# The experts' token rows turned on VectorE, in squares of 32 rows by 32 features written across partition groups, in place of TensorE transposes

## The reference

```python
# x: (2048, 512); 8 experts, 2 picked per token; hidden width F = 1024
x = x + gnn(layernorm(x), adj, ...)            # 2048 x 2048 masked softmax attention
Xf = layernorm(x)                              # (2048, 512)
router_w = softmax(Xf @ Wr)                    # 8 experts
topk_w, topk_idx = top_k(router_w, 2); topk_w = softmax(topk_w)
shared = (silu(Xf @ Wg_s) * (Xf @ Wu_s)) @ Wd_s
gate = silu(einsum('td,edf->etf', Xf, Wg)); up = einsum('td,edf->etf', Xf, Wu)
eout = einsum('etf,efd->etd', gate * up, Wd)
x = x + shared + einsum('etd,te->td', eout, w_full)
```

## Time and profile before

| | |
|---|---|
| median of 3 runs | 1418.66 us (1418.54 to 1420.81) |
| the profiled execution: its time / its span | 1418.73 us / 1417.1 us |
| TensorE busy | 1405.7 us, 99% of the span |
| VectorE busy | 746.4 us, 53% |
| ScalarE busy | 459.2 us, 32% |
| GpSimd busy | 189.5 us, 13% |
| mean granted TensorE clock | 0.999 of full speed (2.4 GHz) |

### The profile page before, as it was taken

How to read it: one execution, slowest core, us unless ns; L and a number is a source line. 1 busy time by engine, 2 the same in 40 slices (tenths; PEclk the granted TensorE clock), 3 DMA queues, 4 the chain that set the end, 5 groups by cost and what they waited for, 6 DMA issues and landing times.

```text
span 1417.1 us, 20076 instructions
## 1 busy us (share of the span) xinstructions
PE 1405.7 (99%) x7084; PEld 1215.3 (86%) x7084; DVE 746.4 (53%) x1557; ACT 459.2 (32%) x732; POOL 189.5 (13%) x234
## 2 busy tenths in 40 slices
PE   8999999999999999999999999999999999999998
PEld 7888888888888888898999889898898989888886
DVE  7955656656666577543243425234252526167874
ACT  4521222221222235343243424334242435243321
POOL 3500111211121133011001010101101010100000
PEclk9999999999999999999999999999999999999999
DMA  5811222322223256272617134261335353553101
GB/s 184 245 38 62 95 75 74 100 85 74 74 78 107 75 181 236 91 221 48 198 30 216 25 74 162 45 201 30 98 133 125 107 131 114 132 159 104 46 15 60
DMA packets 90517, 154.03 MB, mean 109 GB/s; under 512 B 11120, under 2 KB 29552, under 8 KB 88384
## 3 DMA queue, kind: packets, MB, share of 16 engines
q1 hardware_dynamic: 74160, 121.96, 25.5%
q0 software_dynamic: 9760, 18.93, 7.1%
q10 hardware_dynamic: 6528, 12.22, 3.3%
HBM read 114.09 MB, written 40.04 MB: 109 GB/s over the span
## 4 chain that ended last, share of the span: by engine, by line
PE 97%; DVE 1%; DMA 1%; issue 0%; ACT 0%; SPq 0%; POOL 0%; DVEq 0%; ACTq 0%; POOLq 0%
PE bank L279 91%; PE bank L778 2%; PE bank L801 1%; PE bank L982 1%; PE bank L931 1%; PE bank L795 0%; DMA early_x<-x2t 0%; PE bank L727 0%; PE bank L938 0%; DMA wq_raw<-in_L_gnn_W_q_dram 0%; DVE z L1786 0%; SPq L417 0%; PE bank L809 0%; DVE A_l L1396 0%; DVE xq_l L1396 0%
## 5 line engine op out<-in xcount | busy, mean ns | idle before, releaser
L1746 DVE TENSOR_TENSOR hid<-bank,hid 128x384 f32<-128x384 f32 (+1 forms) x80 | 46.7, 584 | 253.4 <-PE bank L279 253.4
L279 PE MATMUL bank<-dn_h,hT_h 128*128 128x512 f32 x416 | 167.9, 404 | 3.2 <-DVE hT_l L1396 3.2
L279 PE MATMUL bank<-dn_h,hT_l 128*128 128x512 f32 x416 | 163.7, 394 | 0.0
L279 PE MATMUL bank<-dn_l,hT_h 128*128 128x512 f32 x416 | 163.2, 392 | 0.0
L279 PE MATMUL bank<-xq_h,gate_h 128*128 128x384 f32 (+1 forms) x320 | 111.3, 348 | 0.1
L279 PE MATMUL bank<-xq_h,gate_l 128*128 128x384 f32 (+1 forms) x320 | 111.2, 347 | 0.0
L279 PE MATMUL bank<-xq_l,gate_h 128*128 128x384 f32 (+1 forms) x320 | 110.8, 346 | 0.0
L279 PE MATMUL bank<-xq_h,up_h 128*128 128x384 f32 (+1 forms) x320 | 110.7, 346 | 0.0
L279 PE MATMUL bank<-xq_h,up_l 128*128 128x384 f32 (+1 forms) x320 | 110.5, 345 | 0.0
L279 PE MATMUL bank<-xq_l,up_h 128*128 128x384 f32 (+1 forms) x320 | 110.4, 345 | 0.0
L279 PE MATMUL bank<-v_h,pT_h 128*128 128x512 f32 x256 | 103.7, 405 | 0.5 <-DVE pT_l L1396 0.5
(11 more groups left out here) (268 smaller groups left out, 3038.0 us busy)
## 6 DMA issues: line engine op xcount, KB each, us to landing
adj_t<-in_adj_dram SPq DMA_DIRECT2D x16, 1024.0 KB, 5.5
gate_raw<-in_L_ffn_Wg_dram SPq DMA_DIRECT2D x16, 1024.0 KB, 6.3
up_raw<-in_L_ffn_Wu_dram SPq DMA_DIRECT2D x16, 1024.0 KB, 9.6
dn_raw<-in_L_ffn_Wd_dram SPq DMA_DIRECT2D x16, 1024.0 KB, 11.5
x_t<-in_x_dram SPq DMA_DIRECT2D x24, 256.0 KB, 7.0
slots<-x2row ACTq DMA_DIRECT2D x12, 512.0 KB, 4.3
e_x<-slots ACTq DMA_DIRECT2D x22, 256.0 KB, 2.8
acc<-x SPq DMA_DIRECT2D x16, 256.0 KB, 2.0
```

What stands on the lines that cost most here:

```text
L279: mm = pe.matmul(o, lhs(a, c), rhs(b, c), start=first and n == 1, stop=last and n == 3 * len(chunks))
L1746: dve.tensor_tensor(hid[:, c % 2, 0:w], bank[2 + c % 2][:, 0:w], hid[:, c % 2, 0:w], ALU.mult).then_inc(sem("hid"), 1)
```

## The change

The transposes L931 of the blocks 1 to 7 (21 tiles) and all of L938 leave TensorE. VectorE turns the rows in squares instead: one instruction reads 32 partitions (rows 32i to 32i+31) and 4 x 32 features of a tile, and writes 32 partitions (32a to 32a+31) of `xq_raw` or of a new tile `tail_raw`. It takes 16 of them, over all (i, a), to turn a tile. In the blocks 2 to 7 the tiles 0 and 1 are turned together, 8 instructions of twice the length in each of the chunks 0 and 1, and tile 2 in the chunks 3 to 6, four instructions in each. In block 1, tile k is turned in the chunks 2+2k and 3+2k, eight in each, and the first tail tile's 16 stand in chunk 1. In a tail tile VectorE begins with the 16 squares of the next one. The copies that followed (`xq_h`, `xq_l`, `tail_xT_h`, `tail_xT_l`) now read SBUF, and stand in other chunks. The wait for `added` moves to the first square. Block 0 still turns its three tiles on TensorE.

```diff
-                return {3: 0, 5: 1, 7: 2}.get(c)
-            return {5: 0, 6: 1}.get(c) if b + 1 < BLOCKS else None
+                return ({4: (0,), 6: (1,), 7: (2,)} if b == 1 else {2: (0, 1), 7: (2,)}).get(c, ())
+            return {5: (0,), 6: (1,)}.get(c, ()) if b + 1 < BLOCKS else ()
+        SQUARES = [(i, a) for i in range(4) for a in range(4)]
+        def turned_in(b, c):
+            if b == 1 and c >= 2:
+                return (c - 2) // 2, 1, SQUARES[c % 2 * 8:][:8]
+            if 1 < b < E:
+                if c < 2:
+                    return 0, 2, SQUARES[c * 8:][:8]
+                if 3 <= c <= 6:
+                    return 2, 1, SQUARES[4 * (c - 3):4 * (c - 2)]
+            return 0, 0, []
+        def tail_turned_in(b, c):
+            return SQUARES if b == 1 and c == 1 else []
...
# TensorE, expert_block
-                    k = prepared_in(b, c)
-                    if k is not None and b + 1 < FIRST_SHARED:
-                        ...
-                        turn_rows(HEAD * b + k, (c + 1) % 2 if b == 0 else 7)
-                    if b == 1 and c == TAIL_IN:
-                        wait(pe, "xq_l", prepared(1) + 2)
-                        turn_tail(1)
+                    if b == 0 and c >= 5:
+                        wait(pe, "silu", c)
+                        turn_rows(c - 5, (c + 1) % 2)
# TensorE, tail_tile
-                if b < E:
-                    wait(pe, "xq_l", prepared(b + 1))
...
                 down(0, range(2, 4))
-                turn_tail(t + 1)
                 down(1, range(0, 4)).then_inc(sem("tail_down"), 1)
# ScalarE: the copies of the high parts read xq_raw and tail_raw; tail_tokens(1) in chunk 2
+                wait(act, "tail_up1", t)
                 tail_tokens(t + 1)
# VectorE
             def next_tokens(b, k, c):
-                    wait(dve, "added", 16 * adds(b - 1) if b > 0 else 0)
...
+            def turn_square(o, rows_, i, a, n=1):
+                return dve.transpose(o[32 * a:32 * a + 32, :, :].rearrange("p c (k q) -> p k c q", k=n)[:, :, :, 32 * i:32 * i + 32],
+                                     rows_[32 * i:32 * i + 32, :, :].rearrange("p k (c f) -> p k c f", c=DC)[:, :, :, 32 * a:32 * a + 32])
+            def turn_rows(b, k, n, squares):
+                for i, a in squares:
+                    if (i, a) == SQUARES[0]:
+                        for q in range(HEAD * b + k, HEAD * b + k + n):
+                            dve.wait_ge(sem(f"e_x_in{q % 2}"), 16 * (q // 2 + 1))
+                        wait(dve, "added", 16 * adds(b - 1))
...
+            def turn_tail(t, squares):
+                    if (i, a) == SQUARES[0]:
+                        wait(dve, "tail_x_in", 16 * t)
+                        wait(dve, "tail_xT_l", t - 1)
...
# VectorE, expert_block
+                    turn_rows(b, *turned_in(b, c))
+                    turn_tail(1, tail_turned_in(b, c))
+                    for k in prepared_in(b, c):
                         next_tokens(b, k, c)
-                    if b == 1 and c == TAIL_IN:
+                    if b == 1 and c == 2:
                         tail_tokens(1)
                     for u, k in todo[1:]:
                         piece(u, k)
# VectorE, tail_tile
+                turn_tail(t + 1, SQUARES)
                 for f in range(2):
```

More of the change, by code:

```diff
@@ L931, in turn_rows @@
                     mm = pe.transpose(bank[to][:, c * P:(c + 1) * P], e_x[:, q % 2, c * P:(c + 1) * P], ident[:])
[L932 to L939, removed]
+                mm.then_inc(sem("x2_turned"), 1)
             def expert_block(b, tail=None):
@@ L1268, in next_tokens @@
                     q = HEAD * b + k
-                    act.wait_ge(sem("rows_turned"), q + 1)
-                    copy(o[:, :, k * P:(k + 1) * P], bank[(c + 1) % 2 if b == 0 else 7][:].rearrange("p (c q) -> p c q", c=DC)
-                         ).then_inc(sem("xq_h"), 1)
+                    part = slice(k * P, (k + 1) * P)
+                    if b == 0:
+                        act.wait_ge(sem("x2_turned"), NT + q + 1)
+                        copy(o[:, :, part], bank[(c + 1) % 2][:].rearrange("p (c q) -> p c q", c=DC)).then_inc(sem("xq_h"), 1)
+                    else:
+                        act.wait_ge(sem("rows_turned"), q + 1 - HEAD)
+                        copy(o[:, :, part], xq_raw[(b + 1) % 2][:, :, part]).then_inc(sem("xq_h"), 1)
                     q += 2
@@ L1759, in next_tokens @@
                 if b + 1 < FIRST_SHARED:
-                    wait(dve, "added", 16 * adds(b - 1) if b > 0 else 0)
                     part = slice(k * P, (k + 1) * P)
-                    minus(o["l"][:, :, part], bank[(c + 1) % 2 if b == 0 else 7][:].rearrange("p (c q) -> p c q", c=DC),
-                          o["h"][:, :, part]).then_inc(sem("xq_l"), 1)
+                    raw = (bank[(c + 1) % 2][:].rearrange("p (c q) -> p c q", c=DC) if b == 0
+                           else xq_raw[(b + 1) % 2][:, :, part])
+                    minus(o["l"][:, :, part], raw, o["h"][:, :, part]).then_inc(sem("xq_l"), 1)
                 else:
@@ L1766, in next_tokens @@
                     minus(o["l"][:, part, :], xq_raw[(b + 1) % 2][:, part, :], o["h"][:, part, :]).then_inc(sem("xq_l"), 1)
+            def turn_square(o, rows_, i, a, n=1):
[7 more added lines that the diff above has]
+                        wait(dve, "added", 16 * adds(b - 1))
+                    q = HEAD * b + k
+                    if n == 2 and q % 2:
+                        rows_ = e_x[:, ::-1, :]
+                    else:
+                        rows_ = e_x[:, q % 2:q % 2 + n, :]
+                    ins = turn_square(xq_raw[(b + 1) % 2][:, :, k * P:(k + n) * P], rows_, i, a, n)
+                    if (i, a) == SQUARES[-1]:
+                        ins.then_inc(sem("rows_turned"), n)
+            def turn_tail(t, squares):
+                tail_rows = tail_x[:].rearrange("p (k d) -> p k d", k=1)
+                for i, a in squares:
+                    if (i, a) == SQUARES[0]:
+                        wait(dve, "tail_x_in", 16 * t)
+                        wait(dve, "tail_xT_l", t - 1)
+                    ins = turn_square(tail_raw[:], tail_rows, i, a)
+                    if (i, a) == SQUARES[-1]:
+                        ins.then_inc(sem("tail_turned"), 1)
             def tail_tokens(t):
                 wait(dve, "tail_xT_h", t)
-                minus(tail_xT["l"][:], bank[7][:].rearrange("p (c q) -> p c q", c=DC), tail_xT["h"][:]).then_inc(sem("tail_xT_l"), 1)
+                minus(tail_xT["l"][:], tail_raw[:], tail_xT["h"][:]).then_inc(sem("tail_xT_l"), 1)
             def results(b):
@@ L1918, in expert_block @@
                         ranks(NT)
-                    k = prepared_in(b, c)
-                    if k is not None:
+                    turn_rows(b, *turned_in(b, c))
+                    turn_tail(1, tail_turned_in(b, c))
+                    for k in prepared_in(b, c):
                         next_tokens(b, k, c)
-                    if b == 1 and c == TAIL_IN:
+                    if b == 1 and c == 2:
                         tail_tokens(1)
```

14 lines of the change are left out of this document (3 added, 11 removed).

## The result

| | before | after |
|---|---|---|
| median | 1418.54 us (20 runs, 1417.04 to 1420.81) | 1421.91 us (20 runs, 1419.22 to 1423.87) |
| ratio | | 1.0024, 95% interval 1.0017 to 1.003 |
| profiled execution, its span | 1418.73 us, 1417.1 us | 1421.79 us, 1420.0 us |

A forecast was written before the change was run, and what follows sets the result against it. The prediction took TensorE to bound the kernel. From 1418.73 us, -5.3 (chunks 3 and 5), 0 (chunk 7), -1.1 (tail tiles), +10.6 (block 1) and +1.0 (its tail tile) gave +5.2, so 1424.0 us, range 1417.5 to 1430.5.

The forecast's parts named there:

- 12 groups in the chunks 3 and 5, blocks 2 to 7: Transpose groups removed from TensorE there are a plain gain: 12 x 0.44 = 5.3 us.
- groups in chunk 7: Blocks 2 to 7: transposes before down(7) only fill its wait for `hT_l`, so removing them gains 0.
- 12 tail tiles: Between the down products, 0.35 of each group's 0.44 us becomes a wait for `hT_l`; 0.09 gained each, 1.1 us in all.
- block 1 to the second matmul of down(7): up(4) stalls 7.0 us because `added` is late, then VectorE's backlog delays down(7): +10.6 us in all.
- its tail tile: Tail tile after block 1: TensorE waits some 1.0 us for hid, behind VectorE's squares and other queued work.
- What bounds it: TensorE, busy 1405.7 of 1417.1 us; work taken from it comes off the time, provided VectorE hands over in time.
- The price of a square: On VectorE, p, the distance of two squares' starts, is 0.32 us without overlap; considered from 0.20 to 0.45.
- in the chunks 4 and 6 a handover [...] 1.6 each: Block 1: ScalarE waits for squares, copies `xq_h`, then makes the piece VectorE's piece needs; 3.2 us for both chunks.
- B: VectorE's squares overlap, start distance 0.20 to 0.26 us: 1418.1 to 1420.5 us, mostly no visible change; chance 0.14.
- C: Block 1: GpSimd's adds end before VectorE reaches the first square, so its wait doesn't hurt: 1413.3 us; chance 0.04.
- D: VectorE's squares are dearer, start distance above 0.38 us: 1428 to 1433 us; chance 0.12.
- E: TensorE's clock falls to half in block 1's two long waits, +4.9 us: 1428.9 us; chance 0.08, atop the main sum.

The follow-up runs named there:

- experiment 5: Changed kernel with block 1's three tiles and all tail tiles but the first turned on TensorE again: 1413.31 us, ratio 0.996 to the kernel before.
- experiment 6: Two runs on the squares' price: changed kernel with squares reordered, 1421.3 us; kernel with block 1's tiles on TensorE, double squares split and short test instructions added, 1410.87 us.
- experiment 3: Changed kernel with block 1's squares moved later, to chunk 3 (behind `up_l`) through chunk 7: 1417.66 us, ratio 0.9999 to the kernel before.
- experiment 2: Changed kernel with `up_l` made ahead of the eight squares in block 1's chunk 2: 1419.29 us, ratio 1.001 to the kernel before.
- experiments 4 and 7: 4: groups put back, 1422.4 us; `hT_l` before `dn_l` in chunk 7, changed kernel 1420.07, kernel before 1417.27. 7: that reorder, block 1's tiles on TensorE, 1407.59.
- the swap on the changed kernel: Changed kernel with VectorE making `hT_l` before the `dn_l` piece in chunk 7 of blocks 1 to 8: 1420.07 us, ratio 1.0012 to the kernel before.
- the other order of squares: Changed kernel with four squares in a row writing the same 32 partitions and reading four different groups: 1421.3 us, ratio 1.0022 to the kernel before.
- the short queues: Changed kernel with block 1's tiles on TensorE, double squares split into pairs, and 32x128 transposes and copies added in block 8: 1410.87 us, one run.
- the swap on the kernel before: Kernel before with VectorE making `hT_l` before the `dn_l` piece in chunk 7 of blocks 1 to 8: 1417.27 us, ratio 0.9991.

## Why the prediction was right, and where its sizes were off

The direction, the mechanism and the place were as forecast. Term by term, from the traces:

| term | forecast | measured |
|---|---|---|
| 12 groups in the chunks 3 and 5, blocks 2 to 7 | -5.3 | -5.2 |
| groups in chunk 7 | 0 | 0 |
| 12 tail tiles | -1.1 | -1.7 |
| block 1 to the second matmul of down(7) | +10.6 | +8.5 |
| its tail tile | +1.0 | +1.3 |
| sum | +5.2 | +2.9 |

(The first measured term is the 6.43 us of blocks 2 to 7 less their nine tail tiles of 0.14, from experiment 5; the third is 12 x 0.14. The spans of the two profiled executions differ by 2.9 us, the medians by 3.4. The rest of 0.5 isn't assigned; it is of the size by which executions of one kernel differ.)

**What bounds it.** Right: TensorE lost 7.9 us of busy time, and the time followed the waits, not the busy sum.

**Chunks 3 and 5, and chunk 7.** Right, 0.42 us a group against 0.44, and nothing in chunk 7, shown by putting groups back in either place. In block 2, up(7) ends at 741.22 and the second matmul of down(7) comes at 744.09, 2.87 us later (2.89 forecast), though the first has to wait now:

```profile
741.22 0.39 PE L281 MATMUL bank<-dn_h,hT_h 128*128 128x512 f32 x1
...
743.79 0.47 PE L281 MATMUL bank<-dn_h,hT_h 128*128 128x512 f32 x1 [0.33 <-DVE hT_l L1400]
744.09 0.39 PE L281 MATMUL bank<-dn_l,hT_h 128*128 128x512 f32 x1
```

Seven such waits of 0.33 us and the 1.66 in block 1 make up what `hT_l` has in the list of waits beyond the 2.9 us it had before.

**Tail tiles.** Right in kind, 0.15 gained in place of 0.09. In block 2's, from the first L985 of the second half to the second matmul of the second down product are 2.35 us (758.65 to 761.00), and were 2.50. So 0.29 of the group's 0.44 became a wait, 0.35 were forecast. It shows in no list of waits, since the matmul in front of it lasts 0.40 us (760.25 to 760.65) and the next starts at 760.66. The step used 0.46 us from `hT_l`'s end to the second matmul; in this place it is 0.40 (760.60 to 761.00).

**The price of a square.** Right in number: 8 squares in 2.51 us, 0.315 apart, with 0.32 forecast; a double one lasts 0.436 us and stands 0.45 from the next (eight in 3.57 us), 0.45 forecast. The reason was incomplete, as experiment 6 shows.

**Block 1.** Right: the wait ended by the DMA of `acc` (9.84 us, some 10 forecast), and up(4) waiting for `up_l` (6.49 us, 7.0 forecast). The term that was mis-sized is the queue behind it, from hid(3) to the end of `hT_l`(7): forecast 28.4 us, measured 26.6 (629.70 to 656.27). The step of it that failed is "in the chunks 4 and 6 a handover [...] 1.6 each". A tile's squares end one chunk before its `xq_h` is wanted. ScalarE copies it meanwhile, and `xq_l` follows the next tile's squares at once:

```profile
637.65 2.50 DVE L1775 STREAM_TRANSPOSE xq_raw<-e_x 32x128 f32<-32x128 f32 x8
640.16 0.69 DVE L1400 TENSOR_TENSOR xq_l<-xq_raw,xq_h 128x512 fp32r<-128x512 f32 x1
640.77 1.22 DVE L1400 TENSOR_TENSOR dn_l<-dn_raw,dn_h 128x1024 fp32r<-128x1024 f32 x1
...
636.60 0.61 ACT L1075 ACTIVATE xq_h<-xq_raw 128x512 fp32r<-128x512 f32 x1
```

So each cost its own 0.61 us and not 1.6, 2.0 us less in the two. Only in chunk 7, where the last tile's squares and its `xq_h` stand together, is there a handover (0.70 us at `xq_l`, 0.26 at `dn_l`). The second wait of TensorE, in front of down(7), was therefore 1.66 us and not 4 to 5. The other part of that difference is TensorE's own work in between, 24.9 us (629.84 to 656.41, less the wait) where 23.0 were forecast, because its clock had fallen (next point).

**The rivals.** B (p near 0.2) is excluded by the 0.315. C (the adds come in time) by the wait of 9.84 us. D by the same 0.315. E is half right. The clock did fall. The windows of TensorE (us, busy with matmuls, granted clock, DMA share, GB/s):

```profile
620.00:624.00 4.00, 3.35 (x18) 1.00 0.35 31
624.00:628.00 4.00, 0.00 (x0) 0.83 0.45 67
628.00:632.00 4.00, 2.16 (x7) 0.50 1.05 400
632.00:636.00 4.00, 4.00 (x18) 0.81 1.05 388
636.00:650.00 14.00, 14.00 (x76) 1.00 0.12 38
```

After the wait at up(4) TensorE ran at the lower of its levels, 1.2 GHz, for some 4 us, its matmuls 0.32 us apart and not 0.17. It cost nothing that can be seen: VectorE, busy without a gap from 625.44, set the pace, and TensorE had time to spare. Behind the second wait, of 1.66 us, there was no fall: its matmuls are 0.23 us apart at once. That such a fall does cost time where TensorE sets the pace is shown by the 1.6 us of experiment 3. The prediction had no row for the clock, but the trace of before had some: in the last stage, behind a wait of 2.90 us, TensorE's matmuls are 0.43 us apart:

```profile
1387.54 0.79 PE L279 MATMUL bank<-dn_h,hT_h 128*128 128x512 f32 x1 [2.90 <-DVE hT_l L1396]
1388.13 0.63 PE L279 MATMUL bank<-dn_l,hT_h 128*128 128x512 f32 x1
1388.56 0.63 PE L279 MATMUL bank<-dn_h,hT_l 128*128 128x512 f32 x1
```

The granted clock there is 0.70 from 1388 to 1392. So the price of a fall could be read before the change, already behind a shorter wait; the prediction's 0.08 was given without these rows. The Trainium skill, "TensorE: Matmul & The Clock Gate", closing table of rules, warns of idle gaps between bursts; the fall after 6.49 us agrees with it.

## What to carry to other kernels

A wait for a slow DMA costs nothing as long as only patient work stands behind it; before you move the instruction that holds it, list what is queued behind the new place and when each of those is due, and then ask whether the engine has the time for the backlog at all, since moving one item ahead (experiment 2) mostly passes the wait to the next. Work taken off the bounding engine is worth its time only where that engine would not wait anyway; a reorder on the other engine that shortens the wait may be what makes it pay (experiments 4 and 7). When a general change has one bad place, look for the exception: here block 1 left as it was turned 3.4 us of loss into 8 us of gain.

## What the hardware showed that was not expected

Holding works on the side that is read as well: three copies of 32x128 that read another group of 32 partitions each time stand 0.22 us apart, those that stay stand 0.13 apart. So in a transposition by squares each square pays its full duration, in either of the two orders tried, and the longer instruction is the remedy: by start distances, 256 elements take 0.45 us where two of 128 take 0.19 + 0.315 = 0.51 us (pairs) or 0.63 us (single ones).

The fall of the clock did not follow the length of the waits alone. It was there behind waits of 6.49 us (changed kernel) and 4.77 us (`up_l` first), and in experiment 3 behind waits of 2.48 and 2.13 us. There the matmuls behind the second wait read

```profile
663.36 0.58 PE L281 MATMUL bank<-up_h,tail_xT_h 128*128 128x512 f32 x1
663.74 0.63 PE L281 MATMUL bank<-up_l,tail_xT_h 128*128 128x512 f32 x1
664.17 0.63 PE L281 MATMUL bank<-up_h,tail_xT_l 128*128 128x512 f32 x1
```

and stay 0.43 us apart (0.23 is full speed) until 666.7, with a granted clock of 0.63 from 664 to 668. But with the swap on the changed kernel a wait of 2.46 us at the same L985 was followed by no fall (granted clock 1.00 from 668 to 676). And one wait is the same in all twelve profiled executions: 2.90 us (2.89 in one) at `hT_l` in the last stage. Behind it the clock fell in eight of them, before and changed kernel among them, and stayed at 1.00 in four (`up_l` first, the other order of squares, the short queues, the swap on the kernel before). From block 9's first matmul to the end of the span the eight take 193.7 to 194.0 us and the four 192.3 to 192.4. So here a fall costs 1.3 to 1.7 us and comes or not in the same work; it is also a part of the spread between executions of one kernel. The length of a wait alone doesn't decide it, and what does is left open.
